# TensorE's batch tiles of a DLRM tower as a loop of two passes over two tiles, with buffers for two tiles

## What is computed

```python
e = jnp.stack([tbl_0[ids[:, 0]], ..., tbl_25[ids[:, 25]]], axis=1)
combined = jnp.concatenate([e, r_dense_x[:, None, :]], axis=1)
interact = jnp.einsum('bfd,bgd->bfg', combined, combined)
z = interact[:, _TRIU_I, _TRIU_J]
h = jnp.concatenate([z, r_dense_x], axis=1)
h = jnp.maximum(h @ W_top1 + b_top1, 0.0)
h = jnp.maximum(h @ W_top2 + b_top2, 0.0)
y = h @ W_top3
```

## Time and profile before

| | us |
|---|---|
| median of 3 runs | 110.68 (109.79 to 111.02) |
| the profiled execution | 111.06 |
| its span in the profile | 109.2 |
| look-up stage, to the first `gram` | 0 to 54.3 |
| tiles 0 to 3, to the last `y` | 54.3 to 107.6 |

### The profile page before, as it was taken

One profiled execution on the slowest core, in us unless ns is written; L12 is line 12 of the kernel. 1 busy time (PEld: TensorE's weight loads), 2 busy tenths in 40 slices (PEclk: granted clock), 3 DMA queues, 4 the chain that ended last, 5 costly groups with the idle time before them and its releaser, 6 DMA issues.

```text
span 109.2 us, 3405 instructions
## 1 busy us (share of the span) xinstructions
PE 99.5 (91%) x1532; PEld 84.6 (77%) x1532; DVE 57.2 (52%) x113; ACT 34.6 (32%) x59; POOL 68.6 (63%) x72
## 2 busy tenths in 40 slices
PE   6995999999998999999899699999999899756992
PEld 6993888887875887888688599879987798655980
DVE  0069999999999999970200731071204530061130
ACT  5016336708416043222520520153412244201022
POOL 3778777777787787777776777777777760000000
PEclk9999999999999999999999999999999999997699
DMA  2999999656968992112212112212122111000000
GB/s 57 194 381 395 364 388 370 245 186 211 376 228 245 392 305 59 48 54 62 59 53 56 48 50 75 56 48 54 48 75 56 50 48 30 0 6 6 0 0 4
DMA packets 6001, 14.68 MB, mean 134 GB/s; under 512 B 1889, under 2 KB 2913, under 8 KB 5858
## 3 DMA queue, kind: packets, MB, share of 16 engines
q1 hardware_dynamic: 3938, 10.26, 27.1%
q0 software_dynamic: 2048, 4.20, 13.4%
HBM read 14.45 MB, written 0.00 MB: 132 GB/s over the span
## 4 chain that ended last, share of the span: by engine, by line
PE 49%; DVE 36%; DMA 7%; ACT 3%; issue 2%; SPq 1%; DVEq 0%
DVE onehot L470 19%; PE gram_ps L310 13%; PE look_ps L341 11%; DVE low L460 10%; PE look_ps L275 8%; PE look_ps L351 7%; DMA table<-tbl_dram 7%; PE turn_ps L296 5%; DVE dots L478 4%; DVE pairs L492 3%; PE look_ps L321 2%; PE look_ps L333 2%; ACT high L545 1%; PE look_ps L360 1%; ACT vecs L554 1%
## 5 line engine op out<-in xcount | busy, mean ns | idle before, releaser
L254 POOL DMA_INDIRECT rows<-tbl_dram,ids_rows x64 | 67.7, 1058 | 20.4 <-issue 19.2
L275 PE MATMUL look_ps<-onehot,high 128*128 128x512 f32 x88 | 33.7, 401 | 1.4 <-ACT high L545 1.2
L275 PE MATMUL look_ps<-onehot,low 128*128 128x512 f32 x88 | 32.9, 392 | 0.1
L470 DVE TENSOR_SCALAR onehot<-ids_wide,row_ids 128x1024 fp32r<-128x1024 int32 x44 | 30.0, 742 | 5.4 <-DMA ids_wide<-ids_look_dram 5.4
L275 PEld LDWEIGHTS look_ps<-onehot,high 128*128 128x128 f32 x88 | 16.3, 188 | 6.0 <-DVE onehot L470 2.2
L275 PEld LDWEIGHTS look_ps<-onehot,low 128*128 128x128 f32 x88 | 16.5, 188 | 3.8 <-DVE low L460 0.6
L478 DVE STREAM_TRANSPOSE dots<-gram_ps 128x352 f32<-128x352 f32 (+2 forms) x12 | 5.6, 466 | 19.8 <-PE gram_ps L310 19.8
L545 ACT CAST high<-table 128x1024 fp32r<-128x1024 f32 (+1 forms) x10 | 11.3, 1138 | 14.7 <-DMA table<-tbl_dram 14.7
L565 ACT COPY vecs<-turn_ps 128x512 f32<-128x512 f32 x16 | 9.4, 594 | 15.1 <-PE turn_ps L296 15.1
L310 PE MATMUL gram_ps<-vecs 128*27 128x27 f32 x1024 | 12.8, 195 | 1.5 <-ACT vecs L565 0.7
L341 PE MATMUL look_ps<-pairs_t,w_sb 128*128 128x128 f32 x96 | 13.5, 297 | 0.2 <-ACT pairs_t L571 0.2
(11 more groups left out here) (34 smaller groups left out, 49.6 us busy)
## 6 DMA issues: line engine op xcount, KB each, us to landing
table<-tbl_dram SPq DMA_DIRECT2D x6, 512.0 KB, 9.9
ids_wide<-ids_look_dram SPq DMA_DIRECT2D x5, 512.0 KB, 5.1
table<-tbl_dram SPq DMA_DIRECT2D x4, 640.0 KB, 4.9
rows<-tbl_dram,ids_rows POOLq DMA_INDIRECT x64, 4.3
w_sb<-w_dram SPq DMA_DIRECT2D x1, 1024.0 KB, 9.2
w_sb<-w_dram SPq DMA_DIRECT2D x1, 512.0 KB, 7.8
x_rows<-x_dram SPq DMA_DIRECT2D x1, 256.0 KB, 10.5
ids_rows<-ids_gather_dram SPq DMA_DIRECT2D x1, 32.0 KB, 1.9
```

The lines of the kernel that those rows point to most:

```text
L254: nc.gpsimd.indirect_dma_start(rows[:, t * NG + i, :], None, tables[GATHER_FIELDS[i]], bass.IndirectOffsetOnAxis(ap=ids_rows[:, t * NG + i ...
L275: mm = nc.tensor.matmul(look_ps[:, j % 2 * 2 + f, :], weights, onehot[:, (STEP0[j] + k) % RING, f * BATCH:(f + 1) * BATCH], start=(name == ...
L470: nc.vector.tensor_scalar(onehot[:, q % RING, :], ids_wide[:, j % WIDE_HELD, :], row_ids[:, kind(j), k:k + 1], None, ALU.is_equal).then_in ...
```

## The change

TensorE's program for the tiles becomes a loop of two passes (`PASSES`), each over two tiles (`HELD`); the body stands once in the program. ScalarE's and VectorE's programs stay written out. What goes with it:

- `rows` and `vecs` hold two tiles instead of four. What the look-up gives for tiles 2 and 3 goes into a new buffer `known`, and ScalarE's `place_known(t)` copies it into `vecs` when `gram` of tile t - 2 is done. `save_look`, `save_x` and VectorE's last copy are split in two for it.
- GpSimd's gathers of tiles 2 and 3 wait, once for each group of four, until the rows of tile t - 2 have been transposed; a semaphore `gather_begun` counts the last four gathers of every second tile.
- In the body all four `turn`s of tile 1 (`turn_second`) stand in tile 0, and all four of the next pass's first tile (`turn_next`) in tile 1. In the last pass `turn_next` has nothing new to transpose and repeats what it did.
- The two halves of `gram` of the body's second tile follow each other directly; `layer1_dense` comes behind `gram` there.
- `CODE_SHIFT` and the old `keep_clock` go; ahead of the last `turn_second` of each pass stand three groups of three fillers (`FILLERS`), each behind a wait for `gather_begun`.
- The wait for both weight matrices, and for VectorE's first half of the last look-up, stands ahead of the loop.

```diff
-CODE_SHIFT = 9
+HELD = 2
+PASSES = TILES // HELD
+FILLERS = 3
...
-        rows = sb("rows", [P, TILES * NG, D])
+        rows = sb("rows", [P, HELD * NG, D])
...
-        vecs = sb("vecs", [P, BATCH // 2, SLOTS, 2])
+        vecs = sb("vecs", [P, HELD * P // 2, SLOTS, 2])
+
+        known = sb("known", [P, (BATCH - HELD * P) // 2, NL + 1, 2])
...
             for t in range(TILES):
+                h = t % HELD
                 for i in range(NG):
+                    if t >= HELD and i % GROUP == 0:
+
+                        pool.wait_ge(turned, turn_index(t - HELD, i // GROUP) + 1)
...
+                    if h == HELD - 1 and i // GROUP == NGROUPS - 1:
+                        pool.sem_inc(gather_begun, 1)
...
+            def keep_clock():
+
+                for _ in range(FILLERS):
+                    nc.tensor.matmul(gram_ps[:, 0, 0:4 * SLOTS], zeros[:], zeros[:, 0:4 * SLOTS],
+                                     start=True, stop=True)
+
+            def turn_second(r, g):
+
+                pe.wait_ge(turn_saved, r * (HELD * NGROUPS) + turn_index(1, g) - 1)
+                if g == NGROUPS - 1:
+
+                    for i in range(1, GROUP):
+                        pe.wait_ge(gather_begun, r * GROUP + i)
+                        keep_clock()
+                pe.wait_ge(rows_landed[1][g], r * (16 * GROUP) + 16 * GROUP)
+                turn(turn_index(1, g), 1, g)
+
+            def turn_next(g):
+
+
+                pe.wait_ge(turn_saved, turn_index(2, g) - 1)
+                pe.wait_ge(rows_landed[0][g], PASSES * (16 * GROUP))
+                turn(turn_index(2, g), 0, g)
...
-            for _ in range(CODE_SHIFT):
-                nc.tensor.matmul(gram_ps[:, 0, 0:4 * SLOTS], zeros[:], zeros[:, 0:4 * SLOTS], start=True, stop=True)
             look_up(0)
...
             pe.wait_ge(last_look_saved, 1)
-            gram(0, 0)
-            turn(1, 1)
             pe.wait_ge(w1_landed, 16)
...
             pe.wait_ge(w2_landed, 16)
...
+            with pe.Fori(0, PASSES) as r:
+
+                pe.wait_ge(look_saved, r + COUPLES)
+                pe.wait_ge(turn_saved, r * (HELD * NGROUPS) + turn_index(1, 0))
+                gram(0, 0)
+                layer1_dense(r, 0)
+                turn_second(r, 0)
+                gram(0, 1)
+                turn_second(r, 1)
+                turn_pairs(r, 0, 0)
+                turn_pairs(r, 0, 1)
+                layer1_pairs(r, 0, 0)
+                turn_pairs(r, 0, 2)
+                layer1_pairs(r, 0, 1)
+                layer1_pairs(r, 0, 2)
+                turn_second(r, 2)
+                layer2(r, 0, 0)
+                layer2(r, 0, 1)
+                turn_second(r, 3)
+                layer3(r, 0)
+
+                pe.wait_ge(look_saved, r * 2 + COUPLES)
+                pe.wait_ge(turn_saved, r * (HELD * NGROUPS) + turn_index(2, 0))
+                gram(1, 0)
+                gram(1, 1)
+                layer1_dense(r, 1)
+                turn_pairs(r, 1, 0)
+                turn_next(0)
+                layer1_pairs(r, 1, 0, 0, 1)
+                turn_pairs(r, 1, 1)
+                layer1_pairs(r, 1, 0, 1, N1)
+                turn_pairs(r, 1, 2)
+                layer1_pairs(r, 1, 1)
+                layer1_pairs(r, 1, 2)
+                turn_next(1)
+                layer2(r, 1, 0)
+                layer2(r, 1, 1)
+                turn_next(2)
+                layer3(r, 1)
+                turn_next(3)
...
+            def place_known(t):
+
+                act.wait_ge(gram_done, t - HELD + 1)
+                act.wait_ge(known_saved, 1)
+                act.wait_ge(last_look_saved, 2)
+                at = (t - HELD) * P // 2
+                copy(tile_vecs(t, slice(0, NL + 1)), known[:, at:at + P // 2]).then_inc(look_saved, 1)
```

More of the change, by code:

```diff
@@ L165, in build @@
         look_saved = sem("look_saved")
+        known_saved = sem("known_saved")
         last_look_saved = sem("last_look_saved")
@@ L313, in gram, with layer1_dense, turn_pairs, layer1_pairs @@
                     mm.then_inc(gram_done, 1)
[L315 to L319, removed]
+            def layer1_dense(r, h):
                 for n in range(N1):
                     nc.tensor.matmul(h1_cols(n), w1_sb[:, PAIR_CHUNKS, n * P:(n + 1) * P],
-                                     dense[:, t * P:(t + 1) * P], start=(n % HALF == 0), stop=False,
-                                     skip_group_check=True)
-            def turn_pairs(t, c):
-                pe.wait_ge(pairs_packed, t * PAIR_CHUNKS + c + 1)
-                if c == 1 and t > 0:
-                    pe.wait_ge(y_saved, t)
+                                     dense[:, bass.ds(r * (HELD * P) + h * P, P)],
+                                     start=(n % HALF == 0), stop=False, skip_group_check=True)
+            def turn_pairs(r, h, c):
+                pe.wait_ge(pairs_packed, r * (HELD * PAIR_CHUNKS) + h * PAIR_CHUNKS + c + 1)
+                if c == 0:
+                    pe.wait_ge(last_look_saved, 2)
+                if c == 1:
+                    pe.wait_ge(known_saved, 1)
+                    pe.wait_ge(y_saved, r * HELD + h + 1)
                 if c == 2:
-                    pe.wait_ge(pairs_saved[0], t * 2 + 1)
+                    pe.wait_ge(pairs_saved[0], r * (HELD * 2) + h * 2 + 1)
                 nc.tensor.transpose(turned_pairs(c), pairs[:, c * P:(c + 1) * P], ident[:]).then_inc(pairs_turned, 1)
-            def layer1_pairs(t, c):
-                if c < 2:
-                    pe.wait_ge(pairs_saved[0], t * 2 + c + 1)
-                else:
-                    pe.wait_ge(pairs_saved[1], t + 1)
-                for n in range(N1):
+            def layer1_pairs(r, h, c, n0=0, n1=N1):
+                if n0 == 0:
+                    if c < 2:
+                        pe.wait_ge(pairs_saved[0], r * (HELD * 2) + h * 2 + c + 1)
+                    else:
+                        pe.wait_ge(pairs_saved[1], r * HELD + h + 1)
+                for n in range(n0, n1):
                     mm = nc.tensor.matmul(h1_cols(n), w1_sb[:, c, n * P:(n + 1) * P],
@@ L362, in layer3 @@
                 mm.then_inc(y_done, 1)
-            def keep_clock(count):
-                for _ in range(count):
-                    nc.tensor.matmul(look_ps[:, 1, 0:P], zeros[:], zeros[:], start=True, stop=True)
             pe.wait_ge(zeros_ready, 1)
@@ L566, in save_turn, with save_pairs @@
                      turn_ps[:, n % 2, :].rearrange("p (s b o) -> p b s o", s=GROUP, o=2)).then_inc(turn_saved, 1)
-            def save_pairs(t):
-                for c in range(2):
-                    act.wait_ge(pairs_turned, t * PAIR_CHUNKS + c + 1)
-                    copy(pairs_t[:, c, :], turned_pairs(c)).then_inc(pairs_saved[0], 1)
+            def save_pairs(t, c):
+                act.wait_ge(pairs_turned, t * PAIR_CHUNKS + c + 1)
+                copy(pairs_t[:, c, :], turned_pairs(c)).then_inc(pairs_saved[0], 1)
             def save_h1(t):
```

159 lines of the change are left out of this document (54 added, 105 removed).

## The result

| | before | changed |
|---|---|---|
| median of 4 runs, us | 110.24 (109.62 to 111.02) | 118.18 (117.49 to 118.83) |
| ratio | | 1.072 (1.061 to 1.082) |
| span of the profiled execution | 109.2 | 117.0 |
| first weight load of `gram`, tiles 0 / 2 / 3 | 54.33 / 77.90 / 93.76 | 55.56 / 90.28 / 104.73 |
| instruction packets of TensorE | 12 | 7 |

The change costs 7.9 us; the forecast was 4.8 by the span and 4.3 against the first median. Medians are over all executions and ratios over those with the clock least disturbed, and the profiles of e3, e6 and e7 are of executions in which it fell more often, so I take from them places, stops and packets, not spans.

What follows compares the result with a forecast made beforehand. TensorE, busy 91% of the span, was taken as the bound, with instruction supply stopping it in the tail. Terms added 4.8 us to the 109.2 span: 114.0, or 115.5 as a median, put at 115.0; own range 112.0 to 118.0.

Steps and rivals of the forecast that it cites:

- The start: Ahead of and in the look-up: removing the nine fillers moves no time; `gram` starts near 54.05 instead of 54.33, -0.3.
- The 0.3 gained on VectorE's smaller copy: End of look-up: half of a 0.69 us copy, perhaps 0.4, now suffices, so `gram` starts near 54.05 instead of 54.33.
- The block behind the loop's entry: Tile 0's `gram`: next block ordered only at about 54.0, 3.7 us a block; tile 0's products 2.3 us late.
- Tile 1's run: Tile 1's `gram`, 512 instructions in one run: 4.9 us with a block stall, against 3.6 before, plus 1.3.
- The fall of the clock: Pass 0, behind stops about 2 us long: each drop would cost up to 1.5 us; counted only in the upper end.
- The rivals: Whole kernel: back edge fetches, 124.6, 0.25; faster, 109 or less, 0.17; no change, 0.11; slower, 112 to 118, 0.47.
- Fillers: Ahead of each pass's last `turn`: 18 passes, 1.9 us, covering perhaps 0.4 of layer 2's save; +3.0 net in all.
- Uncovered copies: Around the last `turn`s, `gram` and the branch: copies and packing no longer hidden by other work, +3.5 us.
- The branch back: Between pass 0 and pass 1: costs 0.1 us, code kept, with bounds from about nothing to 4.0.
- the rival: Branch and pass 1: body blocks are not kept and are fetched again, 9.6 us more, 124.6; chance 0.25.
- The tail: Tile 3: stop ahead of `turn_pairs` and the clock's drop go, -3.4 us; `turn_pairs` 1.15 after `gram`'s last load.

Runs made afterwards that it cites:

- e3: The changed kernel with the loop body written out twice instead of a loop, same order, buffers, fillers and repeats; 126.01 us, ratio 1.127 to the kernel before.
- e6: The changed kernel with its eight zero matmuls at the start made 512 columns wide, no instruction moved; 117.27 us, ratio 1.065 to the kernel before.
- e7: The changed kernel with three start matmuls on zeros (12 instructions) ahead of the look-up; 118.34 us, ratio 1.072 to the kernel before.
- e10: The changed kernel with five start matmuls (20 instructions) ahead of the look-up and the three waits moved into the loop body; 114.89 us, run once.
- e4: The changed kernel with the nine start matmuls on zeros (36 instructions) back ahead of the look-up; 114.98 us, ratio 1.041 to the kernel before.
- e1: The changed kernel with the three waits ahead of the loop moved to the body's first lines; 119.49 us, ratio 1.080 to the kernel before.
- e2: The changed kernel without the fillers in the loop and their waits for `gather_begun`; 116.19 us, ratio 1.044 to the kernel before.
- e5: The changed kernel with nine start matmuls ahead of the look-up and no fillers in the loop; 111.83 us, ratio 1.017 to the kernel before.
- e9: The changed kernel with nine start matmuls, no fillers, and the loop body interleaved as before; 110.13 us, ratio 1.002 to the kernel before.

## Why the prediction was right in sign and too small

118.18 lies just above the forecast's own range of 112.0 to 118.0. Each place as forecast and as measured in the changed kernel:

| reached | forecast | measured | added miss |
|---|---|---|---|
| `gram` of tile 0 | 54.05 | 55.56 | +1.5 |
| first `turn_pairs` of tile 0 | 63.1 | 65.14 | +0.5 |
| `gram` of tile 1 | 72.4 | 75.81 | +1.4 |
| `gram` of tile 2, behind the branch | 86.8 | 90.28 | +0.1 |
| `gram` of tile 3 | 101.3 | 104.73 | -0.1 |
| last `y` done | 112.4 | 115.45 | -0.4 |

**The start: wrong.** "The nine fillers at the start ran while tables were loading; taking them away moves no time" is the step that failed. They lay in the gap ahead of the look-up, and on that account I costed them at nothing. With the gap empty full clock came at 14.2 instead of 7.5, and a look-up that keeps TensorE 99% busy from 14.5 on ends 1.24 later; in the four kernels with this start it ends 0.2 to 2.0 later. e6, which fills the gap and moves nothing, has 1.0 of it back in its profile and 0.8 by ratios whose intervals overlap. The table of eleven kernels carries the cause; the size is not measured better than this. The 0.3 gained on VectorE's smaller copy was not there either: the copy took 0.42, but the first load came 0.75 after its start, as before (0.76). In e3, without the loop's entry, it was 0.62, so 0.13 of it is the entry.

**The block behind the loop's entry: right in mechanism, undersized.** The stop came where it was forecast, a half `gram` behind the entry (four loads of `dense` later, since the block begins ten instructions in), and e10 and e4 take it away by having the block ordered before the wait. I took 3.7 a block from bounds of 3.3 and 4.0; from the end of VectorE's copy (55.23) to the end of the stop at `dense` it was 4.3, and 4.2 to the next stop's end. The row of a stopped block, 4.00, was the nearer one for a stretch full of `gram`; the 3.3 came from blocks without a stop. Tile 1's run took 4.7 against 4.9.

**The fall of the clock: named, not summed.** The rivals had one more drop behind two stops for the upper end only. It came, 65.43 to 68.84, 3.4 us at half speed with the multiplies busy 2.75 of 3.30: about 1.4, the miss of the third row. It fell at about the same place in e1 and e2, and from 63.4 on for 6.8 us in e3 and e6; all of these have both stops in tile 0. But so has e7, 1.65 and 0.54 long, and its clock fell only in tile 1 (79.44 to 82.86). Without the first stop it fell behind tile 1's stop in e4 (74.31 to 77.72) and nowhere in the tiles in e5, e9 and e10, though e5 and e10 stop there for 2.08 and 1.87. So a stop of this length often brings a fall and does not always; which do is not settled.

**Fillers: right in cost.** 2.09 us of loads for 18 passes, 72.43 to 74.42, against 1.9; e2 (3 by the ratios) and e5 against e4 (2.7) are near the 3.0 net.

**Uncovered copies: right at the places read.** From the last `turn` to `gram` 1.39 in both passes, against 1.33; last `turn`, copy and branch 1.33 against 1.4. The last `turn` starts at 103.34, 12 us after its rows could have landed by the earlier trace rows; nine were forecast. The sum had 3.5 for copies and packing no longer covered. No run measures that term by itself: e9, which covers them again and in which tile 1's stop shrinks too, wins 1.6.

**The branch back: right.** I took 0.1 with bounds to 4.0 and a chance of 0.25 for code that comes again. No packet follows the one at 85.5, pass 1 has no stop, and its two tiles took 14.45 and 10.7 against 14.5 and 11.1. e3 shows what code that comes anew costs in this order: about 6 us, where the rival had 9.6. The Trainium skill ("Runtime: NRT & Kernel Launch", Instruction fetch mechanics) has a taken branch out of "the current 2-page window" wait for a fetch; this trace disagrees, for a branch back over more than five blocks. Its figure of 128 KiB for TensorE, also in "Advanced Engine Details and Errata" (ISA Cache), would hold the body, and with that the seven packets agree.

**The tail: right in the profile, overcounted for a median.** 1.13 from the last load to `turn_pairs` against 1.15, clock 1.00. The 3.4 taken off, though, was measured in an execution of before with a fall of the clock, and 14 of its 31 later ones had none.

The staircase by ratio: changed +7.9, with nine start matmuls +4.5, also without fillers +1.9, also interleaved +0.2. Each ratio is uncertain by about 0.01, 1 us. The first step holds the start's clock (0.8 by e6, inside that uncertainty) and the shorter stops with the fall of the clock (2.6).

## What to carry to other kernels

Filler matmuls in an idle gap cost no time here and went with an earlier full clock for what follows: before taking them out, look at when full clock is granted and whether the next stage is bound by TensorE. In code dense with small matmuls count the blocks of 256 instructions; a wait just ahead of a boundary delays the block after it, and moving the boundary by 20 instructions (e1 to e10) took away a stop of 1.3 us and shortened all three from 3.5 to 2.5. A loop whose body is kept frees its later passes from that, but it does not pay for an order that leaves copies uncovered.

## What was not expected of the hardware

- **A wait just ahead of a block holds up the block after it.** Boundary some ten instructions behind the wait (changed, e1): next packet at 57.1 and 57.3, behind the wait. Boundary at the wait, within an instruction (e7): 58.0, behind it too. Boundary some ten (e10) or more (e4) ahead of it: 49.0 and 48.8, inside the look-up. That the sequencer orders the next block on entering one fits all five; at which instruction exactly was not tried.
- **Seven packets for 1382 instructions run twice.** Nothing was loaded again on the branch back; a body too large for that was not tried.
- **Executions of one kernel differ by the clock.** 109.5 and 111.2 us, at mean granted clocks of 1.00 and 0.984, in one series of the kernel before. When full clock is granted in the look-up differs as well: 12.2 to 14.4 us in four kernels with the same start, and the look-up's last copy with it, 53.74 to 55.53. What decides it stays open.
